# Second feed-forward matmul fed by DMA transposes in place of TensorE transposes, and a barrier ahead of the weight loads

## The chip, the cores and the metric

One Trainium2 chip, eight cores, the same program on each, one sequence of the batch per core and no traffic between cores. The metric is the device time in microseconds of the slowest core.

## The reference, cut to what matters

```
x = encoding                                       # (8, 4096, 1024) float32, one sequence per core
A = softmax((x @ R) @ x.T + causal_mask)           # 4096 x 4096 per sequence
y = layernorm(x + A @ x)
h = gelu(bitlinear(y, W1, b1))                     # 4096 hidden
out = layernorm(y + bitlinear(h, W2, b2))

def bitlinear(x, W, b):     # ternary weights, 8-bit activations per token
    w_scale = clip(mean(abs(W)));   Wq = clip(round(W / w_scale), -1, 1) * w_scale
    x_scale = clip(max(abs(x), -1)); xq = clip(round(x * 127 / x_scale)) * x_scale / 127
    return xq @ Wq.T + b
```

## The kernel before, in words

A small recording class (`Builder`) writes each engine's instructions in the order in which the Python code calls it, and works out semaphore waits from named regions: `reads` waits for the writers of a region, `writes` for writers and readers, `accum_writes` for readers only. Each queue that issues DMAs has a pool of completion semaphores (seven on SP, seven on GpSimd, five on ScalarE); DMA number k of a queue waits for number k - 7 (or k - 5) before it is issued. `barrier()` makes each engine wait for all that every engine and every queue has been given so far.

**Attention** (up to about 1077 us). 32 tiles of 128 tokens. The activations are held in two bf16 layouts in `bf_big`; the feature-major one comes from 64 DMA transposes of 512 x 128 elements, issued on SP from a bf16 copy in DRAM (`enc_bf`). Beside it VectorE prepares the ternary weights, which GpSimd's queue stores to DRAM (`w1q_h`, `w2q_h`). Each tile's result goes to DRAM as `y1pre_h`.

**The passage.** Both weight matrices, 8 MB each in bf16, are loaded over the attention's activations in `bf_big`: 8 loads of `w1q_h` on SP, then 4 of `w2q_h` on SP and 4 on ScalarE's queue. Before the change these loads name the regions they overwrite (`etm`, `efm`) and wait for those alone; the wait of every engine for the end of the attention is put in by hand behind them (`bar_targets`). The same holds for the bias rows and the first two `y1t` loads on GpSimd's queue.

**Feed-forward** (to about 2391 us). 32 tiles of 128 tokens, software-pipelined by one tile. For tile i:

- `emit_quant(i)` (VectorE) reads `y1t`, makes the 8-bit activations `xq_tm`; `emit_xqT` turns them feature-major with 8 TensorE transposes into two PSUM buffers and 2 ScalarE copies into `xq_fm`.
- `emit_mm1_half(i, half)`: four groups of 8 matmuls of 512 columns and a bias matmul each (L775, L781); ScalarE applies Gelu, VectorE takes the absolute maximum (L790). Two halves.
- `emit_roundh(i)` (VectorE, L796 to L820) rounds the 4096 hidden values into `hq_tm`, which has two buffers.
- `emit_hqT_half(i - 1, half)`: `hq_tm` of the tile before is turned feature-major by 16 TensorE transposes in 4 groups (L575) with one ScalarE copy each (L582), into `hq_fm`, which has **one** buffer. Two halves, one after each half of the first matmul.
- `emit_mm2(i - 1)`: 64 matmuls of 512 columns (L841, L845) and two for the bias (L849, L853), reading `hq_fm`, all into `pav`.
- `emit_epiB(i - 1)`: VectorE joins `pav` and the residual (L864) into `y2st`, which SP stores as `y2pre_h`; ScalarE and VectorE take the statistics.

**The last pass** (from about 2391 us) normalises all tiles: load, one VectorE operation, store.

```
for i in range(NT + 1):
    emit_mm1_half(i, 0);  emit_hqT_half(i - 1, 0)
    emit_quant(i + 1)
    emit_mm1_half(i, 1);  emit_hqT_half(i - 1, 1)
    emit_roundh(i);       emit_xqT(i + 1)
    emit_mm2(i - 1);      emit_epiB(i - 1)
    emit_s1rows(i + 1);   emit_s2rows(i)
```

Of the kernel before, what the change touches and what calls it, by code (L numbers as in the profile page):

```python
# [7 lines left out]
BF16 = mybir.dt.bfloat16  # L8
# [9 lines left out]
ENGINES = ("sync", "scalar", "vector", "tensor", "gpsimd")  # L18
# [142 lines left out]
def build_nc(NT=32, npart=None):  # L161
    T = NT * 128
    D = 1024
    H = 4096
# [4 lines left out]
    nc = bass.Bass("TRN2", target_bir_lowering=False)  # L169
# [5 lines left out]
    b1bc = nc.dram_tensor("b1bc", [128, H], F32, kind="ExternalInput")  # L175
# [7 lines left out]
    r_bfT = nc.dram_tensor("r_bfT", [8, 128, D], BF16, kind="Internal")  # L183
    y1pre_h = nc.dram_tensor("y1pre_h", [T, D], F32, kind="Internal")
    y2pre_h = nc.dram_tensor("y2pre_h", [T, D], BF16, kind="Internal")
    w1q_h = nc.dram_tensor("w1q_h", [D, H], BF16, kind="Internal")
    w2q_h = nc.dram_tensor("w2q_h", [H, D], BF16, kind="Internal")

    BIGW = max(NT * 2048, 65536)
    with stack:  # L190
# [16 lines left out]
        b = Builder(nc, stack)  # L207
# [35 lines left out]
        def hq_tm(s):  # L243
            return bf_med[:, 8192 + 4096 * s:8192 + 4096 * (s + 1)]
# [13 lines left out]
        def y1t(s):  # L258
            off = [4096, 5120, 7168][s]
            return f32_big[:, off:off + 1024]  # L260
# [69 lines left out]
        NG = NT // 4  # L330
# [298 lines left out]
        for oi in range(NT + 1):  # L629
# [32 lines left out]
            if oi >= 1:  # L662
# [1 line left out]
            drain_prep((oi + 1) / (1.0 * NT))  # L664
        drain_prep(1.0)

        bar_targets = [(b.esem[e2], b.count[e2]) for e2 in ENGINES
                       if b.count[e2] > 0] + b._pool_targets()
        b.dma("gpsimd", b1row2, b1bc[0:2, :],
              writes=["b1row2"] + [f"ATG{s}" for s in range(2, 8)]  # L670
              + ["rstage2"])
        b.dma("gpsimd", b2row2, b2bc[0:2, :], writes=["b2row2"])
        b.dma("gpsimd", y1t(0), y1pre_h[0:128, :], reads=["y1h0"],
              writes=["y1t0", "eres0"])
        if NT > 1:
            b.dma("gpsimd", y1t(1), y1pre_h[128:256, :], reads=["y1h1"],
                  writes=["y1t1", "eres1"])
        for d in range(8):
            b.dma("sync", w1tb(d), w1q_h[128 * d:128 * (d + 1), :],
                  reads=["w1qh"],  # L680
                  writes=[f"w1q{d}"] + [f"etm{k}" for k in range(4 * d, 4 * d + 4)])
        for k in range(8):
            dst = bf_big[:, 32768 + 4096 * k:32768 + 4096 * (k + 1)].rearrange(
                "p (r c) -> p r c", r=4)
            src = w2q_h[512 * k:512 * (k + 1), :].rearrange(
                "(r p) c -> p r c", r=4, p=128)
            b.dma("sync" if k % 2 == 0 else "scalar", dst, src,
                  reads=["w2qh"],
                  writes=[f"w2q{4 * k + j}" for j in range(4)]
                  + [f"efm{k}g{g}" for g in range(NG)])  # L690
        for e in ENGINES:
            bw = []
            for sem, val in bar_targets:
                if b.watermark[e].get(id(sem), 0) < val:
                    bw.append((sem, val))
                    b.watermark[e][id(sem)] = val
            if bw:
                b.ops[e].append((bw, None, None))
        b.op("scalar", lambda s: s.activation(lnu[:, 0:NT], uA[:, 0:NT], AF.Ln),
             reads=["uA"], writes=["lnu"])  # L700
        b.op("scalar", lambda s: s.activation(rstdA[:, 0:NT], lnu[:, 0:NT],
# [93 lines left out]
        def emit_roundh(i):  # L795
            b.op("vector", lambda v: v.reduce_max(hsr, habs[:, 0:8], axis=AXX),  # L796
                 reads=["habs"], writes=["hsr"])
            b.op("vector", lambda v: v.tensor_scalar(
                hsr, hsr, EPS, None, ALU.max), reads=["hsr"], writes=["hsr"])
            b.op("vector", lambda v: v.reciprocal(ch, hsr),  # L800
                 reads=["hsr"], writes=["ch"])
            b.op("vector", lambda v: v.tensor_scalar(
                ch, ch, QB, None, ALU.mult), reads=["ch"], writes=["ch"])
            b.op("vector", lambda v: v.tensor_scalar(
                t2, ch, w2si, None, ALU.mult),
                reads=["ch", "w2si"], writes=["t2"])
            b.op("vector", lambda v: v.tensor_copy(s2hl[:, 0:1], t2),
                 reads=["t2"], writes=["s2hl"])
            b.op("vector", lambda v: v.scalar_tensor_tensor(
                s2hl[:, 1:2], t2, 1.0, s2hl[:, 0:1], ALU.mult, ALU.subtract),  # L810
                reads=["t2", "s2hl"], writes=["s2hl"])
            b.op("vector", lambda v, i=i: v.tensor_scalar(
                s2c[:, i % 2:i % 2 + 1], hsr, w2sb, 1.0 / QB, ALU.mult,
                ALU.mult),
                reads=["hsr", "w2sb"], writes=[f"s2c{i % 2}"])
            rd = [f"hb{s}" for s in range(8)]
            b.op("vector", lambda v: v.tensor_scalar(
                hbuf(0, 4096), hbuf(0, 4096), ch, rcd, ALU.mult, ALU.add),
                reads=rd + ["ch", "rcd"], writes=rd)
            b.op("vector", lambda v, i=i: v.tensor_scalar(  # L820
                hq_tm(i % 2), hbuf(0, 4096), rcd, None, ALU.subtract),
                reads=rd + ["rcd"], writes=[f"hqtm{i % 2}"])

        def emit_s2rows(i):
            b.op("tensor", lambda t: t.transpose(  # L825
# [2 lines left out]
            b.op("scalar", lambda s, i=i: s.copy(s2row2(i % 2),  # L828
                                                 ptp[1][0:2, 0:128]),
                 reads=["ptp1"], writes=[f"s2row2{i % 2}"])  # L830

        def emit_hqT_half(i, half):
            sl = i % 2
            for g in range(4 * half, 4 * half + 4):
                tgroup(hq_tm(sl), f"hqtm{sl}", list(range(4 * g, 4 * g + 4)),
                       g % 2, hq_fm[:, 512 * g:512 * (g + 1)], "hq_fm",
                       accum=True)

        def emit_mm2(i):
            for c in range(32):  # L840
# [17 lines left out]
        def emit_epiB(i):  # L858
# [25 lines left out]
            b.dma("sync", y2pre_h[128 * i:128 * (i + 1), :], y2st(i % 2),  # L884
                  reads=[f"y2st{i % 2}"], writes=[f"y2h{i}"])

        emit_quant(0)
        emit_xqT(0)
        emit_s1rows(0)
        for i in range(NT + 1):  # L890
            if i < NT:
                emit_mm1_half(i, 0)
                if i >= 1:
                    emit_hqT_half(i - 1, 0)
                if i + 1 < NT:
                    emit_quant(i + 1)
                emit_mm1_half(i, 1)
                if i >= 1:
                    emit_hqT_half(i - 1, 1)
                emit_roundh(i)  # L900
                if i + 1 < NT:
                    emit_xqT(i + 1)
            elif i >= 1:
                emit_hqT_half(i - 1, 0)
                emit_hqT_half(i - 1, 1)
            if i >= 1:
                emit_mm2(i - 1)
                emit_epiB(i - 1)
            if i < NT:
                if i + 1 < NT:  # L910
                    emit_s1rows(i + 1)
                emit_s2rows(i)
            if i + 2 < NT:
                b.dma("gpsimd", y1t((i + 2) % 3),
                      y1pre_h[128 * (i + 2):128 * (i + 3), :],
                      reads=[f"y1h{i + 2}"], writes=[f"y1t{(i + 2) % 3}"])
# [71 lines left out]
```

How the kernel before makes its waits and increments, by code:

```python
            def go(eng):  # L144
                for waits, fn, incspec in self.ops[name]:
                    for sem, val in waits:
                        eng.wait_ge(sem, val)
                    if fn is None:
                        continue
                    inst = fn(eng)
                    if incspec is not None:
                        inst.then_inc(incspec[0], incspec[1])
```

## Time and profile before

| what | us |
|---|---|
| median of 2 timed runs | 2589.42 |
| the two runs | 2593.72 and 2585.11 |
| the profiled execution, its own time | 2487.37 |
| its span on the slowest core (core 6) | 2485.8 |
| spans of the eight cores | 2466.1 to 2485.8 |
| mean granted TensorE clock of the cores | 0.915 to 0.920 |

The profile is of one execution, whose time is 102 us shorter than the median of the timed runs. The span runs from the first to the last instruction of the core. SPq is SP as an issuer of DMAs. A granted clock of 1.00 is 2.4 GHz, one of 0.50 is 1.2 GHz. Names of buffers stand without their numbers: `f_big` is `f32_big`, `psc` the PSUM banks of the first matmul, `pav` those of the second, `ptp` those of the transposes.

### The profile page before, as it was taken

The page shows a single profiled execution, that of the slowest core. Times are in us where ns is not written, and L with a number is a line of the kernel's source. Part 1 is how long each engine was busy: PE and PEld are TensorE (multiplying, and loading weights), DVE is VectorE, ACT ScalarE, POOL GpSimd, SP SyncE. Part 2 cuts the span into 40 slices and gives each one's busy share as a digit, 9 for nine tenths or more (in the row PEclk, how much of TensorE's full clock was granted, in tenths as well). Part 3 has the DMA queues.
Part 4 walks back from the last instruction along what each step waited for, and adds up shares of the span by engine and source line. Part 5 has one row for each costly group of instructions (what it writes and reads, how often), then busy time and mean ns, then how long its engine had stood idle before and what let it go on. Part 6 is the DMA issues. An engine that isn't in the chain of part 4 may idle for free.

```text
span 2485.8 us, 27566 instructions; the slowest of 8 cores (2466.1 to 2485.8 us)
## 1 busy us (share of the span) xinstructions
PE 1859.4 (75%) x9016; PEld 798.4 (32%) x9016; DVE 973.6 (39%) x1941; ACT 641.5 (26%) x1271; POOL 170.8 (7%) x307
## 2 busy tenths in 40 slices
PE   0166787888797985208989999989999989999930
PEld 0022233333343432003333333433333333333310
DVE  0032232314143332425545454554545545454322
ACT  0022232323232331003323233232322323233210
POOL 2011111101111111210000000000000000000000
PEclk9988898999899998558999999999999999999965
DMA  8866756545656454582000000000000000000038
GB/s 141 171 195 195 214 167 164 171 116 123 146 133 155 121 148 108 145 249 100 26 20 19 26 14 26 13 26 26 14 26 14 26 19 21 26 14 26 5 130 284
DMA packets 124604, 233.82 MB, mean 94 GB/s; under 512 B 52140, under 2 KB 52268, under 8 KB 123438
## 3 DMA queue, kind: packets, MB, share of 16 engines
q0 software_dynamic: 43408, 129.24, 20.7%
q1 hardware_dynamic: 66016, 88.14, 11.2%
q10 hardware_dynamic: 15040, 14.68, 2.2%
q8 instruction: 75, 1.23, 0.2%
q14 instruction: 65, 0.53, 0.1%
HBM read 166.21 MB, written 69.21 MB: 95 GB/s over the span
## 4 chain that ended last, share of the span: by engine, by line
PE 60%; DMA 20%; issue 7%; DVE 6%; ACT 4%; SPq 2%; POOL 1%; DVEq 0%; ACTq 0%; POOLq 0%
PE psc L775 16%; PE pav L841 9%; PE pav L845 9%; PE psc L546 6%; PE ptp L575 5%; DMA bf_med<-r_bfT 4%; PE psc L531 4%; DMA w1q_h<-f_big 4%; PE pav L592 3%; PE psc L781 3%; PE pav L598 3%; DMA w2q_h<-f_big 3%; DMA bf_med<-y2pre_h 3%; ACT bf_med L582 2%; SPq L108 2%
## 5 line engine op out<-in xcount | busy, mean ns | idle before, releaser
L775 PE MATMUL psc<-bf_big,bf_med 128*128 128x512 bf16 x2048 | 492.0, 383 | 3.2 <-DMA bf_big<-w1q_h 2.9
L841 PE MATMUL pav<-bf_big,bf_med 128*128 128x512 bf16 x1024 | 398.1, 389 | 1.9 <-ACT bf_med L582 1.9
L845 PE MATMUL pav<-bf_big,bf_med 128*128 128x512 bf16 x1024 | 396.9, 388 | 0.0
L531 PE MATMUL psc<-bf_big,bf_med 128*128 128x512 bf16 x512 | 153.2, 457 | 210.7 <-DMA bf_big<-enc_bf 108.5
L546 PE MATMUL psc<-bf_big,bf_med 128*128 128x512 bf16 x1152 | 285.8, 393 | 0.0
L575 PE MATMUL ptp<-ident,bf_med 128*128 128x128 bf16 x1808 | 170.4, 223 | 131.8 <-ACT bf_med L582 63.9
L786 ACT ACTIVATE f_big<-psc,stats 128x512 f32<-128x512 f32 x256 | 176.0, 687 | 346.2 <-PE psc L781 342.2
L790 DVE TENSOR_REDUCE stats<-f_big 128x1 f32<-128x512 f32 x256 | 169.4, 682 | 229.4 <-ACT f_big L786 229.4
L775 PEld LDWEIGHTS psc<-bf_big,bf_med 128*128 128x128 bf16 x2048 | 181.7, 98 | 236.2 <-issue 54.4
L559 ACT ACTIVATE bf_med<-psc,stats 128x512 bf16<-128x512 f32 x144 | 99.2, 689 | 379.7 <-DVE psc L554 183.9
L575 PEld LDWEIGHTS ptp<-ident,bf_med 128*128 128x128 bf16 x1808 | 118.7, 99 | 209.4 <-issue 178.1
L554 DVE TENSOR_TENSOR psc<-psc,mask_sb 128x512 f32<-128x512 f32 x32 | 22.3, 696 | 417.0 <-PE psc L546 325.0
L582 ACT COPY bf_med<-ptp 128x512 bf16<-128x512 bf16 x320 | 172.2, 587 | 23.0 <-PE ptp L575 10.1
L592 PE MATMUL pav<-bf_big,bf_med 128*128 128x512 bf16 x228 | 90.0, 395 | 108.1 <-ACT bf_med L585 96.2
L869 ACT ACTIVATE f_big<-bf_med 128x1024 f32<-128x1024 bf16 x32 | 33.8, 1056 | 519.1 <-DVE bf_med L864 499.2
L864 DVE SCALAR_TENSOR_TENSOR bf_med<-pav,stats,f_big 128x1024 bf16<-128x1024 f32 x32 | 41.0, 1283 | 321.0 <-PE ptp L825 278.7
L546 PEld LDWEIGHTS psc<-bf_big,bf_med 128*128 128x128 bf16 x1152 | 114.6, 101 | 136.0 <-issue 16.5
L531 PEld LDWEIGHTS psc<-bf_big,bf_med 128*128 128x128 bf16 x512 | 55.0, 113 | 306.4 <-issue 276.1
L841 PEld LDWEIGHTS pav<-bf_big,bf_med 128*128 128x128 bf16 x1024 | 102.4, 100 | 125.5 <-issue 13.4
L845 PEld LDWEIGHTS pav<-bf_big,bf_med 128*128 128x128 bf16 x1024 | 102.4, 100 | 122.6 <-issue 9.6
L592 PE MATMUL pav<-bf_big,b1b 128*128 128x512 bf16 x300 | 114.8, 383 | 18.4 <-ACT b1b L585 12.8
L781 PE MATMUL psc<-b1b,rows 2*128 2x512 bf16 x256 | 98.6, 385 | 32.4 <-ACT rows L762 32.4
(112 smaller groups left out, 1544.5 us busy)
## 6 DMA issues: line engine op xcount, KB each, us to landing
f_big<-w1t POOLq DMA_DIRECT2D x64, 512.0 KB, 5.6
f_big<-w2t POOLq DMA_DIRECT2D x64, 512.0 KB, 5.1
f_big<-enc POOLq DMA_DIRECT2D x32, 512.0 KB, 6.9
bf_med<-r_bfT SPq DMA_DIRECT2D x64, 256.0 KB, 3.9
y1pre_h<-f_big SPq DMA_DIRECT2D x32, 512.0 KB, 2.9
f_big<-y1pre_h POOLq DMA_DIRECT2D x32, 512.0 KB, 3.9
out<-f_big SPq DMA_DIRECT2D x32, 512.0 KB, 4.1
bf_big<-enc POOLq DMA_DIRECT2D x36, 256.0 KB, 12.4
```

The lines of the kernel that those rows point to most:

```text
L531: lambda t, e=e, d=d, cur=cur, qlo=qlo, bk=bk: t.matmul(psc[bk][:, :], Rcol(cur)[:, 128 * d:128 * (d + 1)], efm(d, qlo, qlo + 512), start= ...
L546: lambda t, e=e, sup=sup, bank=bank, qi=qi: t.matmul(psc[bank][:, :], encR(e)[:, 128 * (qi % 4):128 * (qi % 4 + 1)], efm(e, 512 * sup, 512 ...
L559: s.activation(A_sb(p)[:, 512 * sup:512 * (sup + 1)], psc[bank][:, :], AF.Exp, bias=bcn, accum_out=sums4[:, sup:sup + 1]),
L575: b.op("tensor", lambda t, j=j, bb=bb: t.transpose(ptp[pk][:, 128 * j:128 * (j + 1)], src_ap[:, 128 * bb:128 * (bb + 1)], ident[:, :]), re ...
L582: b.op("scalar", lambda s, n=n: s.copy(dst2, ptp[pk][:, 0:n]), reads=[f"ptp{pk}"], accum_writes=[dst_region])
L592: b.op("tensor", lambda t, j=j, bb=bb, g=g, nb=nb: t.matmul(pav[:, 0:512], ATg(g)[:, 128 * j:128 * (j + 1)], etm(bb)[:, 0:512], start=(bb ...
L775: b.op("tensor", lambda t, d=d, s4=s4, sup=sup: t.matmul(psc[s4][:, :], xq_fm[:, 128 * d:128 * (d + 1)], w1tb(d)[:, 512 * sup:512 * (sup + ...
L781: b.op("tensor", lambda t, s4=s4, sup=sup, i=i: t.matmul(psc[s4][:, :], s1row2(i % 2), b1row2[:, 512 * sup:512 * (sup + 1)], start=False, ...
L786: b.op("scalar", lambda s, s4=s4, sup=sup, i=i: s.activation(hbuf(512 * sup, 512 * (sup + 1)), psc[s4][:, :], AF.Gelu, scale=s1c[:, i % 2: ...
L790: b.op("vector", lambda v, sup=sup: v.reduce_max(habs[:, sup:sup + 1], hbuf(512 * sup, 512 * (sup + 1)), axis=AXX, apply_absolute_value=True),
L841: b.op("tensor", lambda t, c=c: t.matmul(pav[:, 0:512], hq_fm[:, 128 * c:128 * (c + 1)], w2tb(c)[:, 0:512], start=(c == 0), stop=False), r ...
L845: b.op("tensor", lambda t, c=c: t.matmul(pav[:, 512:1024], hq_fm[:, 128 * c:128 * (c + 1)], w2tb(c)[:, 512:1024], start=(c == 0), stop=False),
```

## The change

Two parts.

**1. The hidden activations are turned by DMA.** `emit_hqT_half` goes, with its TensorE transposes and ScalarE copies. At the end of `emit_roundh(i)` SP stores `hq_tm` (128 x 4096 bf16, 1 MB) to a new DRAM tensor `hq_h`, and `emit_hqTdma(i - 1)`, called after the first half of the first matmul, issues 32 DMA transposes of 128 x 128 on SP from `hq_h` into `hq_fm`.

**2. The passage waits first.** The hand-made wait goes; `b.barrier()` stands ahead of all loads, and these no longer name what they overwrite. The first two `y1t` loads are issued behind the bias loads as before.

```
-        bar_targets = [(b.esem[e2], b.count[e2]) for e2 in ENGINES
-                       if b.count[e2] > 0] + b._pool_targets()
-        b.dma("gpsimd", b1row2, b1bc[0:2, :],
-              writes=["b1row2"] + [f"ATG{s}" for s in range(2, 8)]
-              + ["rstage2"])
+        b.barrier()
+        b.dma("gpsimd", b1row2, b1bc[0:2, :], writes=["b1row2"])
...
             b.dma("sync", w1tb(d), w1q_h[128 * d:128 * (d + 1), :],
-                  reads=["w1qh"],
-                  writes=[f"w1q{d}"] + [f"etm{k}" for k in range(4 * d, 4 * d + 4)])
+                  reads=["w1qh"], writes=[f"w1q{d}"])
...
-        for e in ENGINES:
-            bw = []
-            for sem, val in bar_targets:
...
             b.op("vector", lambda v, i=i: v.tensor_scalar(
                 hq_tm(i % 2), hbuf(0, 4096), rcd, None, ALU.subtract),
                 reads=rd + ["rcd"], writes=[f"hqtm{i % 2}"])
+            b.dma("sync", hq_h[128 * (i % 2):128 * (i % 2 + 1), :],
+                  hq_tm(i % 2), reads=[f"hqtm{i % 2}"],
+                  writes=[f"hqh{i % 2}"])
+
+        def emit_hqTdma(i):
+            for c in range(32):
+                b.dma("sync", hq_fm[:, 128 * c:128 * (c + 1)],
+                      hq_h[128 * (i % 2):128 * (i % 2 + 1),
+                           128 * c:128 * (c + 1)],
+                      reads=[f"hqh{i % 2}"], accum_writes=["hq_fm"],
+                      transpose=True)
...
-        def emit_hqT_half(i, half):
-            sl = i % 2
-            for g in range(4 * half, 4 * half + 4):
-                tgroup(hq_tm(sl), f"hqtm{sl}", list(range(4 * g, 4 * g + 4)),
-                       g % 2, hq_fm[:, 512 * g:512 * (g + 1)], "hq_fm",
-                       accum=True)
...
                 emit_mm1_half(i, 0)
                 if i >= 1:
-                    emit_hqT_half(i - 1, 0)
+                    emit_hqTdma(i - 1)
                 if i + 1 < NT:
                     emit_quant(i + 1)
                 emit_mm1_half(i, 1)
-                if i >= 1:
-                    emit_hqT_half(i - 1, 1)
```

How it moves instructions. On TensorE (PE), one steady tile of the feed-forward, before (line 575 transposes, 775 and 781 first matmul, 841 and 845 second):

```order
L781 MATMUL psc<-b1b,rows 128x512
L575 MATMUL ptp<-ident,bf_med 128x128 x16
L775 MATMUL psc<-bf_big,bf_med 128x512 x8
L781 MATMUL psc<-b1b,rows 128x512
...
L781 MATMUL psc<-b1b,rows 128x512
L575 MATMUL ptp<-ident,bf_med 128x128 x24
L841 MATMUL pav<-bf_big,bf_med 128x512
```

The same place now (line 576 is the transpose, 758 and 764 the first matmul, 828 the second):

```order
L764 MATMUL psc<-b1b,rows 128x512
L758 MATMUL psc<-bf_big,bf_med 128x512 x8
L764 MATMUL psc<-b1b,rows 128x512
...
L764 MATMUL psc<-b1b,rows 128x512
L576 MATMUL ptp<-ident,bf_med 128x128 x8
L828 MATMUL pav<-bf_big,bf_med 128x512
```

The 16 transposes between the halves and 16 of the 24 behind them are gone; the 8 of `xq` stay.

On SP, from the last weight load on, with the semaphores that each DMA waits for (`es_` an engine's, `dp_` a DMA's of that queue), before:

```order
L110 DMA bf_big<-w2q_h 128x4x1024 [waits dp_sync2]
L110 DMA y2pre_h<-bf_med 128x1024 [waits es_scalar,es_vector,dp_gpsimd4,dp_gpsimd6,dp_sync3]
L110 DMA y2pre_h<-bf_med 128x1024 [waits dp_sync4,es_vector]
L110 DMA y2pre_h<-bf_med 128x1024 [waits dp_sync5,es_vector]
```

And now, the same queue around the first `y2pre_h` store:

```order
L108 DMA_TRANSPOSE bf_med<-hq_h 128x128 [waits dp_sync6]
L108 DMA_TRANSPOSE bf_med<-hq_h 128x128 [waits dp_sync0]
L110 DMA hq_h<-bf_med 128x4096 [waits dp_sync1,es_vector]
L110 DMA y2pre_h<-bf_med 128x1024 [waits dp_sync2,es_vector]
L108 DMA_TRANSPOSE bf_med<-hq_h 128x128 [waits dp_sync3,dp_sync1,es_tensor]
L108 DMA_TRANSPOSE bf_med<-hq_h 128x128 [waits dp_sync4]
L108 DMA_TRANSPOSE bf_med<-hq_h 128x128 [waits dp_sync5]
```

Where one store stood per tile there are now 32 transposes, the `hq_h` store and the `y2pre_h` store, in this order; the first transpose of a tile stands behind the `y2pre_h` store of the second matmul before, and waits for TensorE and for its own `hq_h` store.

The loads of the passage keep their place on SP; what they wait for changes. Before:

```order
L110 DMA bf_big<-w1q_h 128x4096 [waits dp_sync5,dp_gpsimd3,dp_gpsimd5,dp_gpsimd1,dp_gpsimd0,dp_gpsimd2,dp_gpsimd4,dp_gpsimd6,es_tensor]
L110 DMA bf_big<-w1q_h 128x4096 [waits dp_sync6]
```

Now:

```order
L110 DMA bf_big<-w1q_h 128x4096 [waits es_scalar,es_vector,es_tensor,dp_sync0,dp_sync1,dp_sync2,dp_sync3,dp_sync4,dp_sync5,dp_sync6,dp_gpsimd0,dp_gpsimd1,dp_gpsimd2,dp_gpsimd3,dp_gpsimd4,dp_gpsimd5,dp_gpsimd6]
L110 DMA bf_big<-w1q_h 128x4096 x6
```

The first load now waits for the last instruction of every engine and the last DMA of every queue.

## Rows read from the trace of the kernel before

**Rows 1.** The page, busy time per engine, and the chain by engine.

```profile
PE 1859.4 (75%) x9016; PEld 798.4 (32%) x9016; DVE 973.6 (39%) x1941; ACT 641.5 (26%) x1271; POOL 170.8 (7%) x307
PE 60%; DMA 20%; issue 7%; DVE 6%; ACT 4%; SPq 2%; POOL 1%; DVEq 0%; ACTq 0%; POOLq 0%
```

**Rows 2.** Windows: length, busy us (instructions) of PE, PEld, DVE, ACT, POOL; PEclk, DMA share, GB/s.

```profile
519.00:520.00 1.00, 1.00 (x9) 0.54 (x8) 0.00 (x0) 0.61 (x2) 0.00 (x0) 1.00 0.52 117
...
1616.00:1656.00 40.00, 36.17 (x185) 15.35 (x182) 20.42 (x46) 12.69 (x23) 0.74 (x2) 1.00 0.06 21
1656.00:1695.00 39.00, 35.65 (x176) 15.30 (x177) 18.70 (x39) 11.60 (x22) 0.32 (x1) 0.96 0.06 21
```

**Rows 3.** Timeline, SP: stores of tiles 0, 12, 30 and 31 (start, duration).

```profile
1184.53 0.33 SPq L110 DMA_DIRECT2D y2pre_h<-bf_med  x1
...
1655.34 0.32 SPq L110 DMA_DIRECT2D y2pre_h<-bf_med  x1
...
2364.26 0.32 SPq L110 DMA_DIRECT2D y2pre_h<-bf_med  x1
...
2390.59 0.32 SPq L110 DMA_DIRECT2D y2pre_h<-bf_med  x1
```

**Rows 4.** Timeline, TensorE, one tile: the transposes and what follows.

```profile
1624.74 0.62 PE L575 MATMUL ptp<-ident,bf_med 128*128 128x128 bf16 x8
...
1626.92 1.89 PE L775 MATMUL psc<-bf_big,bf_med 128*128 128x512 bf16 x8
...
1635.51 0.62 PE L575 MATMUL ptp<-ident,bf_med 128*128 128x128 bf16 x8
...
1638.90 0.38 PE L841 MATMUL pav<-bf_big,bf_med 128*128 128x512 bf16 x1
...
1674.05 0.39 PE L781 MATMUL psc<-b1b,rows 2*128 2x512 bf16 x1
```

**Rows 5.** Timeline around tile 0's end and tile 1's start.

```profile
1138.11 0.61 PE L575 MATMUL ptp<-ident,bf_med 128*128 128x128 bf16 x8 [0.51 <-DVE bf_med L754]
1138.59 1.07 ACT L582 COPY bf_med<-ptp 128x512 bf16<-128x512 bf16 x2 [0.20 <-PE ptp L575]
...
1142.60 0.27 PE L825 MATMUL ptp<-ident,hl 128*2 128x128 bf16 x1 [3.07 <-DVE stats L812]
1142.80 3.59 PE L775 MATMUL psc<-bf_big,bf_med 128*128 128x512 bf16 x8
...
1144.79 2.35 DVE L820 TENSOR_SCALAR bf_med<-f_big,stats 128x4096 bf16<-128x4096 f32 x1
...
1146.86 2.38 PE L775 MATMUL psc<-bf_big,bf_med 128*128 128x512 bf16 x7
...
1168.16 0.38 PE L841 MATMUL pav<-bf_big,bf_med 128*128 128x512 bf16 x1
```

**Rows 6.** All DMA transposes: issue ns min/median/max; then issue to landing, us.

```profile
L108 SPq DMA_TRANSPOSE bf_big<-enc_bf x64: 1129/1214/7114, 61.6 to 659.1; - x64
...
DMA to landing us min/median/max: 2.6/3.7/26.6
```

**Rows 7.** Timeline, SP: two DMA transposes in a row.

```profile
514.43 1.22 SPq L108 DMA_TRANSPOSE bf_big<-enc_bf  x1
515.74 1.21 SPq L108 DMA_TRANSPOSE bf_big<-enc_bf  x1
```

**Rows 8.** Timeline of the passage: the last weight store, the first loads.

```profile
1075.83 0.54 POOL L110 DMA_DIRECT2D w2q_h<-f_big  x1 [6.71 <-DVE f_big L459]
1077.41 8.72 SPq L110 DMA_DIRECT2D bf_big<-w1q_h  x8
```

**Rows 9.** The page's DMA issues: KB each, median us from issue to landing.

```profile
y1pre_h<-f_big SPq DMA_DIRECT2D x32, 512.0 KB, 2.9
w2q_h<-f_big POOLq DMA_DIRECT2D x32, 256.0 KB, 5.6
bf_big<-w1q_h SPq DMA_DIRECT2D x8, 1024.0 KB, 24.9
```

More of the change, by code:

```diff
@@ L185, in build_nc @@
     y2pre_h = nc.dram_tensor("y2pre_h", [T, D], BF16, kind="Internal")
+    hq_h = nc.dram_tensor("hq_h", [256, H], BF16, kind="Internal")
     w1q_h = nc.dram_tensor("w1q_h", [D, H], BF16, kind="Internal")
@@ L665, in build_nc @@
         drain_prep(1.0)
-        bar_targets = [(b.esem[e2], b.count[e2]) for e2 in ENGINES
-                       if b.count[e2] > 0] + b._pool_targets()
-        b.dma("gpsimd", b1row2, b1bc[0:2, :],
-              writes=["b1row2"] + [f"ATG{s}" for s in range(2, 8)]
-              + ["rstage2"])
-        b.dma("gpsimd", b2row2, b2bc[0:2, :], writes=["b2row2"])
[L673 to L677, printed above, removed]
+        b.barrier()
+        b.dma("gpsimd", b1row2, b1bc[0:2, :], writes=["b1row2"])
+        b.dma("gpsimd", b2row2, b2bc[0:2, :], writes=["b2row2"])
         for d in range(8):
             b.dma("sync", w1tb(d), w1q_h[128 * d:128 * (d + 1), :],
-                  reads=["w1qh"],
-                  writes=[f"w1q{d}"] + [f"etm{k}" for k in range(4 * d, 4 * d + 4)])
+                  reads=["w1qh"], writes=[f"w1q{d}"])
         for k in range(8):
@@ L688, in build_nc @@
                   reads=["w2qh"],
-                  writes=[f"w2q{4 * k + j}" for j in range(4)]
-                  + [f"efm{k}g{g}" for g in range(NG)])
-        for e in ENGINES:
-            bw = []
-            for sem, val in bar_targets:
[L694 to L698, printed above, removed]
+                  writes=[f"w2q{4 * k + j}" for j in range(4)])
         b.op("scalar", lambda s: s.activation(lnu[:, 0:NT], uA[:, 0:NT], AF.Ln),
@@ L885, in emit_epiB @@
                   reads=[f"y2st{i % 2}"], writes=[f"y2h{i}"])
+        b.dma("gpsimd", y1t(0), y1pre_h[0:128, :], reads=["y1h0"],
+              writes=["y1t0"])
+        if NT > 1:
+            b.dma("gpsimd", y1t(1), y1pre_h[128:256, :], reads=["y1h1"],
+                  writes=["y1t1"])
         emit_quant(0)
@@ L903, in build_nc @@
             elif i >= 1:
-                emit_hqT_half(i - 1, 0)
-                emit_hqT_half(i - 1, 1)
+                emit_hqTdma(i - 1)
             if i >= 1:
```

## The prediction

> **What bounds the kernel now.** I read the page first: TensorE is busy for 75% of the span and carries 60% of the chain that ended last [rows 1]. Then the windows over the feed-forward, where the first part of the change acts: in each tile TensorE is busy for some 36 of 39 to 40 us, VectorE for half of them, ScalarE for 12, and the DMA engines for 6% of the time [rows 2]. So TensorE bounds this stage and the DMA engines have room. The length of a tile comes from the `y2pre_h` stores, one per tile: tile 0's is issued at 1184.53, tile 30's at 2364.26, so (2364.26 - 1184.53) / 30 = **39.3 us** [rows 3].
>
> Two questions decide the change: how much of TensorE's time goes, and whether 32 DMA transposes per tile come through SP in time.
>
> **What is removed.** In one tile the first 16 transposes stand from 1624.74 to 1626.92, 2.2 us; the 24 behind the second half from 1635.51 to 1638.90, 3.4 us [rows 4]. The 8 that stay (`xq`) cost about 1.6 us when alone, 1138.11 to 1139.66, where their ScalarE copies end [rows 5]. So 2.2 + 3.4 - 1.6 = 4.0 us per tile leave TensorE, and its own floor becomes 39.3 - 4.0 = 35.3 us. If all else were hidden, 31 tiles would give 124 us.
>
> **What is added: a chain through SP.** `hq_fm` has one buffer. The transposes for the next second matmul may not write it before the present one has read it, and on SP they stand behind that matmul's `y2pre_h` store, which waits for VectorE's L864. So for each tile there is a loop: store issued, 32 transposes, second matmul, L864, store. What does not fit into it makes TensorE wait. Its terms:
>
> - From the first matmul of the second product to the end of the store's issue: tile 0, 1168.16 to 1184.53 + 0.33 = 1184.86, **16.7 us** at full clock [rows 3, 5].
> - From the store to the first transpose 0.1 us, the gap between two issues on this queue (515.74 - 514.43 - 1.22 = 0.09) [rows 7].
> - 31 steps from one transpose to the next, of length c. No transpose of 128 x 128 is in the trace. Those of 512 x 128 hold the queue for 1.21 us at the median and follow each other every 1.31 us [rows 6, 7]. A plain DMA holds it for 0.32 us, 0.42 with the gap [rows 3, 7]. These are the two bounds: c lies between **0.42 and 1.31 us**. The DMA engines do not set it: a 512 x 128 transpose is 128 KB, and at the pace of 1.31 us their share is about half [rows 2]; a quarter of the bytes takes a quarter of that. I take the plain DMA's 0.32 as fixed and let the other 0.89 us go with the rows moved: 0.32 + 0.89 / 4 = 0.54, with the gap **c = 0.64**. The value is a choice in the lower half of the range, since it supposes that issuing costs more for more rows.
> - The last transpose lands 2.6 us after its issue starts, the shortest landing of the larger kind [rows 6]; a smaller one may take less.
> - The seven semaphores of SP allow seven DMAs in flight; with landings of 2.6 us that is one per 0.37 us and does not bind at c = 0.64. With landings over 4.5 us it would.
>
> Sum without the clock: 16.7 + 0.1 + 31 x 0.64 + 2.6 = 39.2 us, already what a tile takes today.
>
> **The clock.** TensorE is ready for the second matmul earlier. Tile 12's store is issued at 1655.34 + 0.32 = 1655.66, the last bias matmul of the next first product starts at 1674.05, in 0.3 us it is over; without the 2.2 us of the first 16 transposes that is 1672.2, and with the `xq` transposes 1673.7 [rows 3, 4]. That is 18.1 us after the store, while the last transpose lands 0.1 + 19.8 + 2.6 = 22.5 us after it. So TensorE would idle for some 4.4 us in every tile. What such a pause does stands at the start of tile 1: after 3.07 us of idling behind the `xq` transposes, the next 8 matmuls take 3.59 us where 1.89 is usual, and the 7 after them 2.38 where some 1.7 is [rows 4, 5]: 2.4 us in all, the granted level being the lower one, 1.2 GHz; with the bias matmul between them I take **2.6 us**. The second matmul would begin in that state. The loop is then 39.2 + 2.6 = **41.8 us**, 2.5 us more than now. Today's tiles lose less: one in three or so shows a granted clock of 0.96 [rows 2].
>
> **The ends of the feed-forward.** Tile 0: its rounding ends at 1144.79 + 2.35 = 1147.1; the 1 MB store must land before the transposes. No row has it alone: 512 KB lands in 2.9 us, a 1 MB load among eleven others in 24.9 [rows 9]. I take 4 us. The second product of tile 0 starts at 1147.1 + 4 + 22.5 = 1173.6, not at 1168.16: 5.4 us later, 8 with the clock [rows 5]. In later tiles this store is off the path: it is issued during the second matmul and has over 10 us to land. Tile 31: today it follows tile 30 by 26.3 us, since no first product lies between [rows 3]; the loop of 41.8 us does not get shorter by that: 15.5 us more. Middle: 30 tiles x 2.5 = 76 us.
>
> **The passage.** Today the loads begin at 1077.41; the last `w2q_h` store is issued at 1075.83 and lands some 5.6 us later, at 1081.4 [rows 8, 9]. With the barrier ahead, all loads start then: 4 us later. It could be nothing, if the load's first transfers only wait for each other, and at most some 10 us. What covers the loads today is nothing, since every engine waits for the end of the attention anyway.
>
> **Sum.** 4 + 8 + 76 + 15.5 = 103.5, say 104 us, on the profiled execution's own 2487.4: 2591 us. The timed runs are 102 us longer than this execution. If that is TensorE's time stretched, the new loop suffers less from it, since some 22 of its 42 us are SP's. Spread over 1859 us of TensorE, 102 us are 5.5%; on some 19 us per tile that leave the path this is at most 1 us, 31 us in all; I take half. So 2589.4 + 104 - 15 = **2680 us** (rounded).
>
> **Two rules against each other.** The share of the DMA engines at 117 GB/s of transposes beside little else was 0.52 [rows 2]. The Trainium skill, Advanced Engine Details and Errata, section X-Bar Transpose (TRN2), says that transposing DMAs are as fast as regular ones, at 350 to 400 GB/s. By it the 1 MB of a tile would be an estimated 3 us and all would be hidden; the trace agrees that bandwidth is not the limit, but shows that issuing is. The Trainium skill, VectorE: DVE Perf Modes, section The three transpose paths, gives 1309 ns for a 128 x 128 transpose by DMA against 390 ns on TensorE. If that is time on the queue, c would not fall with the size, which is the first rival below; the trace has 1.31 us only for 512 x 128.
>
> **Rivals.**
> 1. *A transpose's issue costs the same at any size.* For it: the only size in the trace shows 1.31 us [rows 7]. Against it: nothing but that a plain DMA of 256 KB is issued in 0.32 [rows 3], so the cost belongs to the transposing and may go with its parts. Then the loop is 16.7 + 0.1 + 31 x 1.31 + 2.6 + 2.6 = 62.6 us: 30 x 23.3 = 699, tile 0 29, tile 31 36, passage 4: +768, or about **3340 us**.
> 2. *SP keeps up* (the other side). If a small transpose costs hardly more than a plain DMA, c = 0.42, the last lands 15.7 us after the store, before TensorE's 18.1, and TensorE's floor holds: 30 x -4.0 = -120, tile 31 about 3 us more, passage 4, tile 0 nothing: **2475 us**. It decides from c = 0.48 down, where the time would be over 2% lower.
> 3. *The loop holds but costs nothing to speak of*: c near 0.56, or the pause does not lower the clock. With c = 0.64 and no clock term, 30 x -0.1 = -3, with the ends +24 or so: **2600 us**, within 2%.
> 4. *Landings grow* under the `hq_h` and `y1t` traffic, so that the seven semaphores bind: median landing 3.7 us today [rows 6]; with 7 us, c = 1.0 and +356 us: **2930 us**.
>
> **How the numbers follow.** Each 0.01 us in c is worth 32 x 31 x 0.01 = 9.9 us, so c carries the range. Chances: the forecast (c from 0.6 to 0.9) 0.50; rival 3 (c from 0.48 to 0.6, or no clock term) 0.24; rival 1 0.14; rival 4 0.06; rival 2 0.06. 2% is 52 us, about what a measurement of this kernel can tell from no change. Faster 0.06, same 0.24, slower 0.70. The range reaches from c = 0.49 (2680 - 15 x 9.9 = 2530, a little above it as TensorE's floor comes near: 2540) to c = 0.92 (2960); it leaves out rival 1 and most of rival 2, 0.2 in all.
>
> **What would show it.** Right: the spacing of the 128 x 128 transposes on SP near 0.64 us; SP busy for 20 us of each tile; TensorE waiting some 4 us for a DMA into `bf_med` before the first matmul of each second product, at a granted clock of 0.50 for a few us behind it; tiles of 41.8 us; the loads starting about 4 us after today's. Wrong: a spacing of 1.2 to 1.3 us with tiles above 60 (rival 1), tiles of 35 with no wait for a DMA (rival 2), a spacing near 0.64 with no drop of the clock (rival 3), or SP waiting for its own transposes to land (rival 4).

## The result, and the profile after

| | median us | runs |
|---|---|---|
| the kernel before | 2503.77 | 10 runs, 2486.12 to 2593.72 |
| the changed kernel | 3235.09 | 11 runs, 3223.84 to 3266.71 |
| ratio | 1.297 | 95% interval 1.292 to 1.302 |

Some executions of every kernel here are some per cent longer, with a lower granted clock on the cores of one die or both; the ratios, and all times below this table, leave them out.

The change costs 30%: 731 us between these medians, 740 us between the spans of the two profiled executions. The forecast was 2680 us in a range of 2540 to 2960; the time lies outside it and 105 us below the first rival's 3340.

The page of the changed kernel, busy time per engine and the chain by engine, answers to [rows 1]:

```profile
PE 1808.9 (56%) x7834; PEld 747.3 (23%) x7992; DVE 971.7 (30%) x1941; ACT 507.8 (16%) x1015; POOL 172.4 (5%) x307
SPq 39%; PE 30%; DMA 18%; issue 7%; DVE 5%; ACT 1%; POOL 1%; DVEq 0%; another core or an unknown queue 0%; ACTq 0%; POOLq 0%
```

SP as an issuer of DMAs had 2% of the chain and now has 39%; TensorE fell from 60% to 30%. In a window about as long as one tile, TensorE is now busy for 34 of 60 us, and the DMA engines for 16% of it (the last three numbers are granted clock, DMA share and GB/s; compare [rows 2]):

```profile
2060.00:2120.00 60.00, 34.23 (x145) 13.65 (x148) 19.63 (x42) 7.92 (x14) 0.53 (x1) 0.78 0.16 48
```

What holds the chain is one group, the transposing DMAs on SP (count, issue ns min/median/max). The line below it has the time from issue to landing, over these and the 32 `hq_h` stores together. It answers to [rows 6]:

```profile
L108 SPq DMA_TRANSPOSE bf_med<-hq_h x1024: 1093/1185/2334, 1163.9 to 3111.2; - x171
...
DMA to landing us min/median/max: 2.2/2.3/6.8
```

A transpose of 128 x 128 holds the queue for 1.185 us at the median, one of 512 x 128 held it for 1.214: a quarter of the rows, 2% less time. SP's timeline over a tile, stores and transposes (start, duration), against [rows 3, 7]:

```profile
2006.94 0.47 SPq L110 DMA_DIRECT2D hq_h<-bf_med  x1
2026.56 0.33 SPq L110 DMA_DIRECT2D y2pre_h<-bf_med  x1
2027.08 41.28 SPq L108 DMA_TRANSPOSE bf_med<-hq_h  x32
2068.53 0.45 SPq L110 DMA_DIRECT2D hq_h<-bf_med  x1
2088.07 0.33 SPq L110 DMA_DIRECT2D y2pre_h<-bf_med  x1
```

32 transposes in 41.28 us, so 1.29 us from one to the next, and 2088.07 - 2026.56 = 61.5 us from store to store. SP's waits between 1250 and 3000 us are all for VectorE's L851, that is for the result which the `y2pre_h` store carries (in us: total, times, longest; L147 is the helper's line that waits), and none is for a DMA of its own to land:

```profile
SPq L147 <- DVE bf_med L851: 535.8, 28, 20.2
```

TensorE's timeline in the same tile, the last work before the wait and the first behind it, against [rows 4]:

```profile
2043.64 0.61 PE L576 MATMUL ptp<-ident,bf_med 128*128 128x128 bf16 x8 [0.16 <-DVE bf_med L737]
...
2069.98 0.59 PE L828 MATMUL pav<-bf_big,bf_med 128*128 128x512 bf16 x1 [25.73 <-DMA bf_med<-hq_h]
```

TensorE is through with its other work at 2044.3 and waits 25.7 us for the last transpose. Over the run the page's group of that line has 786 us of such idle time, nearly all put down to one releaser:

```profile
L828 PE MATMUL pav<-bf_big,bf_med 128*128 128x512 bf16 x985 | 406.4, 413 | 786.2 <-DMA bf_med<-hq_h 785.9
```

**Where the 740 us of span come from.** The first and the last stores bound the parts (timeline of SP, before in [rows 3]):

```profile
1224.44 0.33 SPq L110 DMA_DIRECT2D y2pre_h<-bf_med  x1
...
3070.99 0.33 SPq L110 DMA_DIRECT2D y2pre_h<-bf_med  x1
...
3132.36 0.34 SPq L110 DMA_DIRECT2D y2pre_h<-bf_med  x1
```

| part | before | after | difference |
|---|---|---|---|
| to tile 0's store | 1184.53 | 1224.44 | 39.9 |
| 30 tiles | 1179.7 (39.3 each) | 1846.6 (61.55 each) | 666.8 |
| tile 31 | 26.3 | 61.4 | 35.0 |
| last pass | 95.2 | 93.1 | -2.1 |
| span | 2485.8 | 3225.5 | 739.7 |

Of the first 39.9 us, 9.1 lie in the attention, which the change does not touch: its last store is issued at 1085.67 in this execution and core, at 1076.59 before. The loads follow it after 4.2 us, where 0.8 us lay between before [rows 8]. From the first load to tile 0's store it is 134.6 us against 107.1 before, 27.5 more: that is tile 0, whose 32 transposes stand before its second product too. The lines of the passage, now:

```profile
1085.67 0.32 SPq L110 DMA_DIRECT2D y1pre_h<-f_big  x1
...
1089.83 8.41 SPq L110 DMA_DIRECT2D bf_big<-w1q_h  x8
```

### The profile page after: what moved, and what is told of

Read it like the earlier page. It is cut to its first block, busy times and chain, and to the rows that moved or that the text cites. A ratio compares the mean times of both kernels' runs of the same rounds, so it can differ in the third digit from the quotient of the medians.

```text
span 3225.5 us, 27053 instructions; the slowest of 8 cores (3199.4 to 3225.5 us)
## 1 busy us (share of the span) xinstructions
PE 1808.9 (56%) x7834; PEld 747.3 (23%) x7992; DVE 971.7 (30%) x1941; ACT 507.8 (16%) x1015; POOL 172.4 (5%) x307
## 4 chain that ended last, share of the span: by engine, by line
SPq 39%; PE 30%; DMA 18%; issue 7%; DVE 5%; ACT 1%; POOL 1%; DVEq 0%; another core or an unknown queue 0%; ACTq 0%; POOLq 0%
SPq L108 38%; PE pav L832 8%; PE pav L828 8%; PE psc L547 5%; DMA bf_med<-r_bfT 4%; PE psc L532 3%; PE pav L593 3%; DMA w2q_h<-f_big 3%; PE pav L599 3%; DMA bf_med<-hq_h 2%; DMA bf_med<-y2pre_h 2%; DMA w1q_h<-f_big 2%; DMA f_big<-w1t 1%; DVE bf_med L851 1%; DMA bf_big<-w1q_h 1%
## 5 line engine op out<-in xcount | busy, mean ns | idle before, releaser
L828 PE MATMUL pav<-bf_big,bf_med 128*128 128x512 bf16 x985 | 406.4, 413 | 786.2 <-DMA bf_med<-hq_h 785.9
L832 PE MATMUL pav<-bf_big,bf_med 128*128 128x512 bf16 x1017 | 419.0, 412 | 60.9 <-DMA bf_med<-hq_h 57.5
L851 DVE SCALAR_TENSOR_TENSOR bf_med<-pav,stats,f_big 128x1024 bf16<-128x1024 f32 x32 | 41.1, 1284 | 1089.9 <-PE ptp L819 927.6
L828 PEld LDWEIGHTS pav<-bf_big,bf_med 128*128 128x128 bf16 x1024 | 107.4, 105 | 987.7 <-issue 888.2
L593 PE MATMUL pav<-bf_big,bf_med 128*128 128x512 bf16 x221 | 88.1, 398 | 109.3 <-ACT bf_med L586 89.0
L832 PEld LDWEIGHTS pav<-bf_big,bf_med 128*128 128x128 bf16 x1024 | 106.5, 104 | 138.4 <-issue 37.3
L593 PE MATMUL pav<-bf_big,b1b 128*128 128x512 bf16 x293 | 112.1, 383 | 19.5 <-ACT b1b L586 17.0
L110 POOL DMA_DIRECT2D f_big<-y1pre_h x32 | 17.0, 532 | 1841.1 <-DVE stats L862 1841.1
L599 PE MATMUL pav<-bf_big,b1b 128*128 128x512 bf16 x294 | 112.5, 383 | 4.5 <-PE ptp L576 0.4
L576 PE MATMUL ptp<-ident,bf_med 128*128 128x128 bf16 x784 | 73.4, 221 | 59.2 <-DMA bf_big<-w1q_h 51.8
```

The lines of the kernel that those rows point to most:

```text
L593: b.op("tensor", lambda t, j=j, bb=bb, g=g, nb=nb: t.matmul(pav[:, 0:512], ATg(g)[:, 128 * j:128 * (j + 1)], etm(bb)[:, 0:512], start=(bb ...
L599: b.op("tensor", lambda t, j=j, bb=bb, g=g, nb=nb: t.matmul(pav[:, 512:1024], ATg(g)[:, 128 * j:128 * (j + 1)], etm(bb)[:, 512:1024], star ...
L828: b.op("tensor", lambda t, c=c: t.matmul(pav[:, 0:512], hq_fm[:, 128 * c:128 * (c + 1)], w2tb(c)[:, 0:512], start=(c == 0), stop=False), r ...
L832: b.op("tensor", lambda t, c=c: t.matmul(pav[:, 512:1024], hq_fm[:, 128 * c:128 * (c + 1)], w2tb(c)[:, 512:1024], start=(c == 0), stop=False),
```

## The experiments

Two theories stood against each other after the result. **Theory 1**: a transposing DMA costs its queue about 1.2 us as an instruction, whatever it moves. **Rival 2**: the cost goes with the groups of 128 source columns, and only the rows are free; the two kernels have one such group in every transpose, so both theories fit them. Four more questions were open: the share of the passage, the loop through the one `hq_fm`, the clock, and whether the transposing or the waits make the spacing.

### The passage alone

`e1_barrier_only`: the kernel before, with only the second part of the change.

```
+        b.barrier()
+        b.dma("gpsimd", b1row2, b1bc[0:2, :], writes=["b1row2"])
...
-        for e in ENGINES:
-            bw = []
```

> The kernel before with the second part of the change alone (barrier() ahead of the loads, the first two y1t loads behind it). Theory A (the passage is a small term): the loads start 4 us after the last y1pre store lands, time within 2 to 12 us above before. Rival B (the passage carries a good part of the 735 us, by overlap that it loses): 50 us or more above before.

Measured: 2498.69 us beside 2493.23 for the kernel before, ratio 1.0018 with an interval of 1.0005 to 1.0031, that is 4.5 us (1 to 8). In its trace SP issues the last `y1pre_h` store at 1082.40 and the first weight load at 1086.40, 4.0 us later:

```profile
1082.40 0.32 SPq L110 DMA_DIRECT2D y1pre_h<-f_big  x1
1086.40 6.67 SPq L110 DMA_DIRECT2D bf_big<-w1q_h  x8
```

Theory A holds for the size; the passage is a small loss. The expectation counted 4 us from the landing of the last `y1pre_h` store; they count from its issue. It lands 3.5 us after its issue, and SP's last wait before the load (1.4 us) is for that landing. The prediction had named the last `w2q_h` store.

### The DMA transposes alone

`e2_dma_only`: the changed kernel with the passage of before.

> The changed kernel with the passage of before put back, so the DMA transposes alone. Theory A: within 2 to 12 us below the changed kernel, that is some 725 to 735 us above before, tiles of 61.5 us, 32 transposes in 41.2 us of SP per tile. Rival B: 50 us or more below the changed kernel.

Measured: 3226.70 us, ratio 1.294 (1.292 to 1.296) against the changed kernel's 1.297 (1.292 to 1.302). Theory A holds: the difference of some 8 us is no more than the intervals allow, and agrees with the passage alone. The first part of the change carries all but a few of the 740 us.

### The same bytes in fewer instructions

`e3_16_of_128x256` and `e4_4_of_128x1024`: 16 transposes of 256 columns, or 4 of 1024, in place of 32 of 128. For the second:

```
-            for c in range(32):
-                b.dma("sync", hq_fm[:, 128 * c:128 * (c + 1)],
+            for c in range(4):
+                b.dma("sync", hq_fm[:, 1024 * c:1024 * (c + 1)].rearrange(
+                          "p (g r) -> p g r", r=128),
                       hq_h[128 * (i % 2):128 * (i % 2 + 1),
-                           128 * c:128 * (c + 1)],
+                           1024 * c:1024 * (c + 1)],
```

> The changed kernel with 16 DMA transposes of 128 x 256 per tile in place of 32 of 128 x 128. Theory 1 (each transpose costs SP 1.2 us whatever its size): the loop is 16.7 + 0.1 + 15 x 1.29 + 2.3 + 2.6 = 41.1 us, about 32 x 20.4 = 650 us below the changed kernel, near 2580. Rival 2 (the cost goes with the groups of 128 columns; rows alone are free): each takes 2.4 us on SP, the tile stays at 61.5 us and the time at about 3235.

> The changed kernel with 4 DMA transposes of 128 x 1024 per tile. Theory 1 (cost per instruction): SP needs 5.2 us per tile, the transposes are done before TensorE is ready, the tile falls to TensorE's floor of 35.3 us and the time to 2380 to 2430 by the profiled execution's 2487, faster than before. Rival 2 (cost by groups of 128 columns): 4 instructions of some 9 us each, tile 60 us, time near 3200.

Measured: 2607.72 us in one run for 16 (the kernel before beside it 2493), and for 4 a median of **2340.00 us, ratio 0.938 (0.936 to 0.940)**: faster than the kernel before, and below the 2380 to 2430 expected. The transposes of both, first of 256 columns, then of 1024 with SP's timeline over a tile:

```profile
L108 SPq DMA_TRANSPOSE bf_med<-hq_h x512: 1167/1198/2682, 1163.8 to 2492.0; - x171
```

```profile
L108 SPq DMA_TRANSPOSE bf_med<-hq_h x128: 1215/1308/3924, 1176.2 to 2230.2; - x128
...
DMA to landing us min/median/max: 3.8/4.5/7.6
...
1714.70 0.33 SPq L110 DMA_DIRECT2D y2pre_h<-bf_med  x1
1715.22 7.63 SPq L108 DMA_TRANSPOSE bf_med<-hq_h  x4
1741.05 0.34 SPq L110 DMA_DIRECT2D hq_h<-bf_med  x1
1748.68 0.33 SPq L110 DMA_DIRECT2D y2pre_h<-bf_med  x1
```

Twice the columns cost 1.198 in place of 1.185 us, eight times the columns 1.31 at the median. Rival 2 falls: by it the four would have needed some 9 us each. Theory 1 stands for the narrow ones; for the wide ones it is short, since the four together hold SP for 7.63 us here and 7.1 us on average over the 32 tiles, not the 5.2 expected. The 16 give a tile of 42.2 us (31 intervals, 1205.0 to 2513.1), 1 us above what was expected. With 4, a tile lasts 1748.68 - 1714.70 = 34.0 us, where 35.3 was expected, and TensorE no longer waits for a transpose; its timeline, from the last transposes of `xq` on:

```profile
1663.84 0.61 PE L576 MATMUL ptp<-ident,bf_med 128*128 128x128 bf16 x8 [0.15 <-DVE bf_med L737]
1664.30 0.38 PE L829 MATMUL pav<-bf_big,bf_med 128*128 128x512 bf16 x1
```

The second product starts 0.5 us after the first of those 8 transposes, and in the window around it the granted clock is the higher level:

```profile
1640.00:1680.00 40.00, 38.45 (x176) 15.73 (x175) 20.26 (x43) 7.91 (x14) 0.53 (x1) 1.00 0.36 97
```

### Is the cost a constant up to any size

`e6_one_wide`: one transpose of 128 x 4096 per tile. `e5_4_wide_old_passage`: 4 of 128 x 1024. Both with the passage of before.

> One DMA transpose of 128 x 4096 per tile, with the passage of before. Theory 1 (a cost per instruction, the rest hidden behind TensorE): the tile stays at TensorE's 34.0 us and the ratio at 0.937. Rival 3 (a wide transpose moves its bytes slowly by itself, four run beside each other): the one lands over 18 us after the store and TensorE waits, tile over 34 us. Rival 2 (cost by column groups): 32 x 1.2 = 38 us on SP.

> 4 DMA transposes of 128 x 1024 per tile with the passage of before (loads ahead of the wait). Sum of the parts as measured: ratio 0.9384 of the run with the new passage less 0.0018 for the passage, so 0.937, tiles of 34.0 us, near 2340 where before is 2494. Rival (the parts are not additive, or the passage hides): the same ratio as with the new passage, 0.938 or above.

Measured: 2343.29 us, ratio 0.941 (0.938 to 0.944), for one; 2341.55 us, ratio 0.939 (0.937 to 0.941), for four. The one wide transpose:

```profile
L108 SPq DMA_TRANSPOSE bf_med<-hq_h x32: 5190/7048/8790, 1185.0 to 2234.4; - x32
```

So theory 1 as it was put, "whatever it moves", ends at the wide ones: the 1 MB in one instruction holds SP for 7.0 us, as long as the four take together (7.1 us on average). At this width the time goes with what is moved and no longer with the count; whether with the bytes or with the groups of 128 columns, these runs do not tell apart. At 32 groups in 7 us the latter would be 0.2 us each and not rival 2's 1.2. Rival 3 falls too: the one transpose lands 9.2 us after its issue at the median, TensorE needs it some 17.6 us after the `y2pre_h` store, and the tile stays at 34.0 us. The four with the old passage are not measurably better than with the new one (0.939 against 0.938, where 0.937 was expected): the 4.5 us of the passage did not show in this pair, and this run is no improvement on `e4_4_of_128x1024`.

### Count or bytes

`e9_half_the_transposes` issues every other transpose of 128 x 128, so that half of `hq_fm` keeps old contents:

```
-            for c in range(32):
+            for c in range(0, 32, 2):
```

> The changed kernel with 16 instead of 32 transposes of 128 x 128 per tile; every other block of hq_fm is left unwritten. Theory 1 (cost per instruction): the same tile as with 16 of 128 x 256, 41 us and SP at 1.29 us per transpose, though half the bytes move. Rival (cost by bytes or column groups beside it): clearly below the run with 16 of 128 x 256, tile under 39 us.

Measured: 2604.38 us (one run), beside 2607.72 (one run) for 16 transposes that move twice as much. SP over a tile:

```profile
1717.86 0.33 SPq L110 DMA_DIRECT2D y2pre_h<-bf_med  x1
1718.38 20.23 SPq L108 DMA_TRANSPOSE bf_med<-hq_h  x16
...
1758.79 0.33 SPq L110 DMA_DIRECT2D y2pre_h<-bf_med  x1
```

16 in 20.23 us are again 1.26 to 1.29 us each, and the tile is 40.9 us here, 41.6 on average. Half the bytes at the same count change the tile by 0.6 us; half the count at the same bytes (42.2 from 61.5) changed it by 19. The count decides.

### The transposing or the waits

`e10_plain_copies` drops `transpose=True`: the same 32 blocks, queue and waits, the blocks arriving unturned.

> The changed kernel with 32 plain DMAs of 128 x 128 in place of the transposing ones (the blocks arrive unturned); same waits, same queue, same bytes. Theory 1 (the 1.2 us belong to the transposing instruction): issue 0.32 to 0.35 us, spacing 0.42, all landed before TensorE is ready, tile 34 us, time near 2350. Rival W (the waits on the seven semaphores make the spacing): spacing stays near 1.3 us and the tile near 61.5.

Measured: 2464.41 us (one run; the kernel before beside it 2508.83, also one run), where some 2350 was expected. The copies and SP's timeline:

```profile
L110 SPq DMA_DIRECT2D bf_med<-hq_h x1024: 319/381/1686, 1198.0 to 2345.8; - x171
...
1709.29 0.32 SPq L110 DMA_DIRECT2D y2pre_h<-bf_med  x1
1709.80 16.29 SPq L110 DMA_DIRECT2D bf_med<-hq_h  x32
```

0.38 us of issue against 1.185, so some 0.8 us per instruction belong to the transposing itself; the waits do not make the spacing of 1.29 (rival W falls). The spacing here is 16.29 / 32 = 0.51 us, not the 0.42 expected, and the tile 36.6 us (1233.9 to 2367.2 in 31), not 34: TensorE still waits for the last copy, 1.8 us per tile between 1300 and 2200 us and 3.2 at most. In this run SP did wait for its own copies to land, 31 us in all in the same stretch of 24 tiles. So the lower end of the range for c, 0.42, was not reached even by plain DMAs.

### The loop through one buffer

`e8_two_hq_fm`: two `hq_fm`, one `hq_tm` in exchange, the `y2pre_h` store on ScalarE's queue.

```
-        hq_fm = bf_med[:, 0:4096]
+        def hq_fm(s):
+            return bf_med[:, 12288 * s:12288 * s + 4096]
...
-            return bf_med[:, 8192 + 4096 * s:8192 + 4096 * (s + 1)]
+            return bf_med[:, 8192:12288]
...
-            b.dma("sync", y2pre_h[128 * i:128 * (i + 1), :], y2st(i % 2),
+            b.dma("scalar", y2pre_h[128 * i:128 * (i + 1), :], y2st(i % 2),
```

> The changed kernel with two hq_fm buffers (and one hq_tm, to fit), the y2pre_h store on ScalarE's queue; still 32 transposes of 128 x 128 on SP. Theory L (a loop: store, transposes, second product, with one buffer): SP no longer waits for the second product, a tile is 41.3 us of transposes, 0.5 us of the hq_h store and its 4.0 us of landing, 46 us, and the time falls by about 31 x 15 = 470 us to near 2760. Rival (no loop, the transposes are starved by something else): tile stays near 61.5 us.

Measured: 2752.78 us in one run, tiles of 46.0 us (1232.4 to 2658.7 in 31), as worked out. SP's timeline:

```profile
1719.53 0.45 SPq L110 DMA_DIRECT2D hq_h<-bf_med  x1
1723.65 40.29 SPq L108 DMA_TRANSPOSE bf_med<-hq_h  x32
1766.72 0.34 SPq L110 DMA_DIRECT2D hq_h<-bf_med  x1
```

SP now goes from one tile's transposes to the next with only the 1 MB store between: its issue, 3.6 us of waiting for its landing, and in half of the tiles some 2 us of waiting for VectorE's rounding. The 15.5 us that went are the second product and its epilogue, which had stood behind the transposes. The loop is real, and with it gone SP's own sequence is the bound: TensorE still waits 9.6 us per tile for it. The run took out two links at once, the single buffer and the place of the `y2pre_h` store on SP ahead of the transposes; which of them holds the loop by itself was not tried.

### The clock

`e7_fill_the_wait` puts 112 matmuls, whose results nobody uses, where TensorE waits.

```
+                emit_fill()
                 emit_mm2(i - 1)
```

> The changed kernel with 112 extra matmuls of 512 columns (24.1 us, results unused) where TensorE waits 25.7 us for the transposes. Theory C (the pause costs the lower clock on the first 8 matmuls, 1.65 us per tile): tile 59.9 us, time some 50 us below the changed kernel, granted clock of the second product 1.00. Rival: the pause costs nothing beyond itself, tile 61.5 us.

In the changed kernel the second product begins at the lower level; windows of 2 us around its start at 2069.98 (granted clock is the third number from the end):

```profile
2068.00:2070.00 2.00, 0.02 (x1) 0.05 (x2) 0.00 (x0) 0.00 (x0) 0.00 (x0) 0.50 0.39 148
2070.00:2072.00 2.00, 2.00 (x5) 0.69 (x6) 0.00 (x0) 0.00 (x0) 0.00 (x0) 0.50 0.96 393
2072.00:2074.00 2.00, 2.00 (x7) 0.76 (x6) 0.00 (x0) 0.00 (x0) 0.00 (x0) 0.66 0.00 0
2074.00:2076.00 2.00, 2.00 (x11) 0.93 (x10) 0.00 (x0) 0.00 (x0) 0.00 (x0) 1.00 0.00 0
```

With the filling the time was 3192.49 us, one run, some 40 us below the changed kernel; but half of that lies outside the tiles, since the attention ended 16 us earlier in this execution. The mean tile is 61.0 us (1207.9 to 3099.4 in 31) against 61.55, a third of the 1.65 us expected. Two things stand in its trace. First, the filling did not close the wait, of which some 1.8 us per tile remained, and in some tiles the clock fell all the same. One such tile, and a window of 60 us that holds the tile behind it, where it did not fall:

```profile
2048.00:2050.00 2.00, 2.00 (x6) 0.71 (x5) 0.00 (x0) 0.00 (x0) 0.00 (x0) 0.50 0.59 238
2060.00:2120.00 60.00, 56.92 (x261) 24.10 (x260) 19.63 (x42) 7.91 (x14) 0.53 (x1) 1.00 0.17 49
```

That sorts the tiles of one execution. From the start of one second product to the start of the next, the 9 that begin at a granted clock of 0.50 to 0.58 (in the first 4 us) take 62.3 us on average, the 22 that begin at 1.00 take 60.5. So the lower clock costs 1.7 us per tile, as theory C has it and as the changed kernel's own rows say: 8 matmuls spaced 0.43 us where 0.215 is usual. Second, the 32 transposes hold SP for 41.9 us on average here, 41.1 in the changed kernel. This 0.7 us per tile took back a good part of the gain; why they are slower beside the filling stays open.

## Why the prediction was wrong

- **The bound, and the loop: right.** The order store, 32 transposes, second product, store set the tile. Its terms against what was measured at 2026.56 to 2088.07:

| term | forecast us | measured us |
|---|---|---|
| store to first transpose | 0.1 | 0.2 |
| 31 steps of c | 19.8 (c = 0.64) | 40.1 (c = 1.29) |
| last issue to the second product | 2.6 | 2.8 |
| second product to the store's end, with the clock | 16.7 + 2.6 = 19.3 | 18.4 |
| tile | 41.8 | 61.5 |

- **The step that failed** is the one where c was chosen: "I take the plain DMA's 0.32 as fixed and let the other 0.89 us go with the rows moved". The cost does not go with the rows. 128 rows cost 1.185 us, 512 rows 1.214; 256 columns 1.198; and half as many transposes take half the time, whether they move the same bytes or half of them. The 20.3 us that this step missed in every tile are the whole miss of 19.7 in the tile, the other terms being 0.6 us too high together; by the same step tile 0 came 27.5 us later and not 8. The prediction had two bounds, 0.42 and 1.31. The nearest row for a transpose was the other transpose, at 1.31; it went down to 0.64 on a supposition that no row supported, and gave the upper bound a chance of only 0.14.
- **Rival 1**, with c = 1.31, was what happened: a tile of 62.6 us forecast and 61.5 measured, 768 us forecast and 740 found in the span. Its sign, a spacing of 1.2 to 1.3 us with tiles above 60, is what the trace shows. It should have been the forecast, or the range should have held it.
- **The base was off as well.** Both timed runs that the forecast started from, 2593.72 and 2585.11, lie some 100 us above the 2493 us that the kernel before takes beside the experiments, near its profiled 2487. The 15 us taken off for them had no ground in a row. Its own terms, 104 us, on the right base give about 2597, so the absolute forecast of 2680 stands some 80 us nearer to the measured time by luck. The same offset, with the 28 us by which its terms were too high, puts rival 1's 3340 above the 3235 measured.
- **The rule that spoke for it.** The row is 1.29 us from one 128 x 128 transpose to the next, of which the issue takes 1.185. The Trainium skill, VectorE: DVE Perf Modes, section The three transpose paths, has 1309 ns for a transpose of this size by DMA. The page does not say whether that is time on the queue; the trace agrees if it is, and not if it is the time to landing, 2.3 us here. By this rule an estimate of 31 x 1.31 us for the term would have been right within 0.5 us. The Trainium skill, Advanced Engine Details and Errata, section X-Bar Transpose (TRN2), speaks of 350 to 400 GB/s. The traces do not agree at either end: 32 KB per 1.29 us are 25 GB/s, and 1 MB in one instruction held SP for 7.0 us, some 150 GB/s.
- **The clock term**: the mechanism was right, the size 2.6 was taken from the start of tile 1, where two groups of matmuls suffered; here it is 1.7, by the changed kernel's rows and by the tiles of `e7_fill_the_wait`.
- **Rival 4** did not occur: a transpose lands 2.3 us after its issue at the median, and SP never waited for one to land. Its time was summed wrongly besides. The 356 us come on top of the forecast, which makes about 3035 us and not 2930; c = 1.0 lies above the 0.92 at which the range ends. So the range left out rival 4 as well.
- **Tile 31** gets no shorter: forecast 15.5 with the tile of 41.8, measured 35.0 with one of 61.4; the step was right, its input not. **The passage**: 4 forecast, 4.5 (1 to 8) measured by itself. The size was right; the wait that ends last is for the last `y1pre_h` store, where the prediction had the last `w2q_h` store, so that the 4 came out right is partly luck. **The `hq_h` store**: 4 forecast, 4.0 measured.
- **TensorE's floor** was put at 35.3 us. It is 34.0, as the kernels with wide transposes show. The term that was mis-sized is the 1.6 us for the 8 `xq` transposes: their ScalarE copies were counted, but TensorE goes on to the second product without them, after 0.5 us. That is 1.1 of the 1.3 us; the rest was not looked into.

## What to carry to other kernels

Count the instructions of a DMA queue, not the bytes: moving transposes from TensorE to 32 small DMAs cost 30%, and the same move in 4 wide ones (128 x 1024, one output block per 128 columns) gained 6% over the kernel before, because the tile lost 5.3 us on TensorE and SP needed 7 us of the 18 it had. The bytes come in again with wide transposes: 1 MB takes 7 us in one instruction or in four. Before a term rests on how a cost scales, look whether any row varies that size; where none does, the forecast takes the nearest row of the same kind and the range holds both ends. And a buffer that is single, filled from a queue on which the store of the result stands first, puts the filling behind the reading: 15.5 us per tile here, shown by taking away both.

## What the runs showed of the hardware

- A transposing DMA on SP holds the queue for 1.19 us at 128 x 128, 1.21 at 512 x 128, 1.20 at 128 x 256, 1.31 and 1.41 at 128 x 1024 in two kernels (medians), and for 7.0 at 128 x 4096. Four of 128 x 1024 in a row hold it for 7.1 to 7.5 us together on average, 1.8 to 1.9 us each. A plain DMA of 128 x 128 holds it for 0.38, one of 1 MB for 0.32 to 0.47. What limits the wide ones to some 150 GB/s, these runs do not name. Why the small ones share a floor near 1.1 to 1.2 us was not settled either: it is not the waits and not the bytes.
- 32 plain DMAs of 128 x 128 in a row on SP come every 0.47 to 0.56 us, some waiting for earlier ones to land, slower than the 0.42 that two rows had suggested.
- A pause of some 25 us before the second product costs 1.7 us behind it: the first 8 matmuls run at a granted clock of 0.50. Behind pauses of 0.7 to 3.1 us in `e7_fill_the_wait` the clock fell in 8 of 30 tiles, not always behind the longest.
- A store of 1 MB by SP, alone, lands after 4.0 us (the page of the changed kernel: `hq_h<-bf_med`, 32 issues).
